# Moving the expert layer, the B, C and z products and the result products to other steps of the unit in a pipelined last stage

## The reference

```python
t = _unfold3(t, 2).transpose(0, 2, 1)          # taps of a 3x3 window, stride 2
h = t @ proj_w.T + proj_b                      # 768 channels

def _ssm_forward(x, A, W_B, b_B, W_C, b_C, W_D, b_D, p_Delta):   # x = layernorm(h)
    Bproj = x @ W_B + b_B                      # 16 states
    Cproj = x @ W_C + b_C
    delta = softplus(x @ W_D + b_D + p_Delta)  # x @ W_D is the "z product"
    A_bar = exp(delta[..., None] * A)
    B_bar = (A_bar - A) / (delta[..., None] * A) * delta[..., None] * Bproj[:, :, None, :]
    h = a * h + b * xl[..., None]              # per step of the sequence
    y = einsum('bn,bdn->bd', c, h)

route_prob = softmax((x @ enc_w + enc_b) @ sw_w + sw_b)   # x = layernorm(h) again, 8 experts
hid = gelu(einsum('td,edr->ter', x, w1) + b1) * onehot(argmax(route_prob))
out = (einsum('ter,erd->td', hid, w2) + onehot @ b2) * max(route_prob)
```

## Time and profile before

| what | value |
|---|---|
| runs | 9088.94, 9092.56, 9096.12 us; median 9092.56 |
| profiled execution | 9095.32 us, its span 9093.5 us |
| mean granted TensorE clock | 0.914 |
| PE busy | 7714.0 us, 85% |
| POOL busy | 6188.6 us, 68% |
| DVE busy | 6128.7 us, 67% |
| ACT busy | 4307.8 us, 47% |
| last stage, POOL's first product to the end of its last | 3644.8 to 8993.0 us |

### The profile page before, as it was taken

How to read it: one execution, slowest core, us unless ns; L and a number is a source line. 1 busy time by engine, 2 the same in 40 slices (tenths; PEclk the granted TensorE clock), 3 DMA queues, 4 the chain that set the end, 5 groups by cost and what they waited for, 6 DMA issues and landing times.

```text
span 9093.5 us, 86859 instructions
## 1 busy us (share of the span) xinstructions
PE 7714.0 (85%) x31228; PEld 3228.1 (35%) x31228; DVE 6128.7 (67%) x6499; ACT 4307.8 (47%) x7641; POOL 6188.6 (68%) x2484
## 2 busy tenths in 40 slices
PE   6799999876999996588888888788888888888887
PEld 4444444322434432133333333333333333333333
DVE  1255555542233333888888888888888888888885
ACT  1366666553344442444544445444445444454442
POOL 0011111115766640999999999999999999999995
PEclk8999999998999997699888998899998899988988
DMA  0011111113544432223333323233232332233331
GB/s 25 18 45 42 41 44 39 32 32 82 104 97 98 100 68 63 98 100 104 111 114 111 109 91 123 96 121 109 100 116 98 115 119 100 95 119 105 113 114 49
DMA packets 356855, 786.60 MB, mean 87 GB/s; under 512 B 70437, under 2 KB 282806, under 8 KB 348936
## 3 DMA queue, kind: packets, MB, share of 16 engines
q1 hardware_dynamic: 320376, 690.75, 24.9%
q0 software_dynamic: 21712, 51.75, 2.3%
q10 hardware_dynamic: 14336, 38.54, 1.2%
HBM read 597.36 MB, written 183.35 MB: 86 GB/s over the span
## 4 chain that ended last, share of the span: by engine, by line
PE 33%; DVE 14%; ACT 5%; issue 5%; POOL 3%; DMA 0%; SPq 0%; DVEq 0%; ACTq 0%; POOLq 0%
PE ps L1527 7%; PE ps L1635 6%; DVE v L1880 6%; DVE v L1871 5%; PE ps L1534 5%; PE ps L1532 5%; PE ps L1573 3%; ACT ps L1762 3%; PE ps L1523 2%; POOL v L1482 2%; PE ps L1638 2%; PE ps L1636 2%; POOL v L1494 1%; PE ps L1577 1%; DVE dl L1861 1%
## 5 line engine op out<-in xcount | busy, mean ns | idle before, releaser
L1880 DVE TENSOR_TENSOR_SCAN v<-ps,v 128x898 f32<-128x898 f32 x1344 | 2725.5, 2028 | 92.4
L1482 POOL TENSOR_TENSOR v<-xr,bt 128x1792 f32<-128x1792 f32 x672 | 2690.0, 4003 | 98.4 <-DMA xr<-h_by_channel 98.4
L1494 POOL TENSOR_TENSOR v<-v,ct 128x1792 f32<-128x1792 f32 x672 | 2475.4, 3684 | 239.6 <-ACT st L1723 238.9
L1762 ACT ACTIVATE ps<-dr,aa 128x448 f32<-128x448 f32 x2688 | 1586.0, 627 | 1554.8 <-DVE v L1880 1537.7
L1871 DVE SCALAR_TENSOR_TENSOR v<-ps,aa,v 128x448 f32<-128x448 f32 x2688 | 1691.2, 671 | 560.5 <-ACT ps L1762 501.0
L222 POOL DMA_DIRECT2D tokens<-ob x448 | 236.3, 534 | 1889.9 <-ACT ob L383 1839.1
L1635 PE MATMUL ps<-w_or_w,gm 128*112 128x384 f32 x1792 | 721.9, 552 | 369.7 <-DVE gm L1957 277.1
L1573 PE MATMUL ps<-v,dg 128*32 128x448 f32 x5376 | 705.1, 599 | 212.8 <-POOL v L1494 122.9
L1635 PEld LDWEIGHTS ps<-w_or_w,gm 128*112 128x112 f32 x1792 | 334.5, 197 | 768.5 <-DVE gm L1957 319.5
L1527 PE MATMUL ps<-h,w_or_w 128*128 128x448 f32 x1344 | 536.2, 549 | 16.6 <-DVE gm L1924 16.6
L1532 PE MATMUL ps<-x,wpa 128*128 128x448 f32 x1008 | 445.5, 577 | 17.3 <-ACT h L1688 10.1
(11 more groups left out here) (324 smaller groups left out, 11951.0 us busy)
## 6 DMA issues: line engine op xcount, KB each, us to landing
xr<-h_by_channel SPq DMA_DIRECT2D x168, 896.0 KB, 5.6
dr<-delta_by_channel SPq DMA_DIRECT2D x168, 896.0 KB, 6.3
x<-tokens SPq DMA_DIRECT2D x252, 224.0 KB, 5.3
tokens<-ob POOLq DMA_DIRECT2D x448, 112.0 KB, 2.4
w_or_w<-in_w SPq DMA_DIRECT2D x29, 1536.0 KB, 6.4
w_or_w<-centred_w SPq DMA_DIRECT2D x27, 1536.0 KB, 6.4
h_by_channel<-h SPq DMA_DIRECT2D x112, 336.0 KB, 10.9
delta_by_channel<-dl SPq DMA_DIRECT2D x112, 336.0 KB, 4.5
```

Source lines behind the costliest of these rows:

```text
L1482: tt(v[:, n % RING, :, 1:T + 1], xr[:, dc % 2], bt[:, q:q + 1, :].to_broadcast([128, 4, T]), ALU.mult).then_inc(s_v, 1)
L1494: tt(v[:, n % RING, :, 1:T + 1], v[:, n % RING, :, 1:T + 1], ct[:, q:q + 1, :].to_broadcast([128, 4, T]), ALU.mult).then_inc(s_cm, 1)
L1762: fn(decay(g), dr[:, dc % 2, g, :], ACT.Exp, scale=aa[:, 4 * k + g:4 * k + g + 1]).then_inc(s_a, 1)
L1880: nc.vector.tensor_tensor_scan(row, flat[:, 1024 * pair:1024 * pair + 2 * T + 2], row, 0.0, ALU.mult, ALU.add).then_inc(s_sc, 1)
```

## The change

No operation is added or removed. Thirty-odd numbers of the table change, and with them the step at which parts of `mlp` and `front` are issued, and three places in SP's loop. The taps (P_PJ, P_MU, A_HW, A_MU) stay where they are.

```diff
-        P_PJ, P_MU, P_VAR, P_Z, P_BC = 1, 7, (8, 10), 11, 9
-        A_HW, A_MU, A_SQ, A_RS, A_MX, A_SP = 5, 11, (9, 13), 14, (16, 17), (17, 18)
-        V_Z, V_BC, V_DL = 15, 14, (18, 19)
-        P_SQ, P_MEAN, P_ENC, P_IN, P_LOG, P_TURN = (0, 2), 1, 4, 5, 6, 10
-        P_MASK, P_OUT = (12, 13, 14, 15), (16, 17, 18, 18, 19, 20, 21, 22)
-        A_SQ2, A_MS, A_RS2, A_EX, A_GL = (2, 4), 5, 7, 11, 14
-        A_OUT = (21, 22, 23, 23, 24, 25, 26, 27)
-        V_VAR, V_ENC, V_IN, V_LOG, V_EQ, V_OH, V_MASK = 6, 8, 9, 10, 12, 14, (16, 17, 18, 19)
-        ROUTE, TAIL = 9, 28
+        P_PJ, P_MU, P_VAR, P_Z, P_BC = 1, 7, (8, 10), 12, 11
+        A_HW, A_MU, A_SQ, A_RS, A_MX, A_SP = 5, 11, (9, 13), 14, (17, 18), (18, 19)
+        V_Z, V_BC, V_DL = 16, 15, (19, 20)
+        P_SQ, P_MEAN, P_ENC, P_IN, P_LOG, P_TURN = (1, 3), 2, 5, 7, 7, 11
+        P_MASK, P_OUT = (14, 15, 16, 17), (18, 19, 20, 20, 21, 22, 23, 23)
+        A_SQ2, A_MS, A_RS2, A_EX, A_GL = (2, 5), 6, 8, 12, 16
+        A_OUT = (23, 24, 25, 25, 26, 27, 28, 28)
+        V_VAR, V_ENC, V_IN, V_LOG, V_EQ, V_OH, V_MASK = 7, 9, 11, 11, 13, 15, (18, 19, 20, 21)
+        ROUTE, TAIL = 9, 29
...
-                    if k == 11 and i >= 1:
+                    if k == 15 and i >= 1:
                         sp.wait_ge(s_hm, MT * i)
                         sp.dma_start(w2, w["w2"]).then_inc(s_wv, 16)
...
-                    if k == 19 and i + 1 < UNITS:
+                    if k == 20 and i + 1 < UNITS:
                         store_delta(i + 1)
-                    if k == 20:
+                    if k == 21:
                         spread(i + 1, 0)
```

## The result

| | before | after |
|---|---|---|
| median of 20 runs each | 9088.82 us (9078.29 to 9101.25) | 9117.12 us (9094.67 to 9126.33) |
| ratio | | 1.0027, 95% interval 1.0021 to 1.0033 |
| profiled execution, its span | 9095.32, 9093.5 us | 9110.96, 9109.2 us |
| first POOL product of the last stage to the end | 5448.7 us | 5470.1 us |
| unit, mean of units 2 to 26 | 191.73 us | 192.30 us |

The kernel is slower by 0.27%, 28 us by the medians; 9119 was forecast. The halves are means over 24 or 25 units, taken between the same instructions as in the prediction: the DVE half from the first weighing of step 12 (L1871) to the end of the fourth masking (L1957), the PE half from there to the end of the taps of the means, shown by ACT's copy behind them (L1691). The change moves 53 numbers of the table, more than the thirty-odd that are named above.

The account below looks back on a forecast made before the run. A ring of DVE and PE halves, not POOL, bounds the unit: 80.4 + 112.1 = 192.5 us against 191.7. 9095.3 + 20 (25 units) + 7 (edges) = 9122, less 2.8 to the median: 9119 us; range 9060 to 9165.

Parts of the forecast that it names:

- the DVE half: First weighing of step 12 to last masking on DVE: forecast 80.4 us a unit, 18.8 more than 61.6.
- the PE half: First result product to end of the means' taps: forecast 110.0 us, 112.1 with 2.1 to the weighing, 18.0 less.
- The ring: DVE half and PE half set the unit, 191.7 us before, 192.5 forecast; POOL's 9.3 us idle is left over.
- A: Rival: gaps at steps 12 and 13 go, nothing replaces them; unit 185.3, about 8930 us; with milder form 17%.
- B: Rival: no change, halves cancel or the clock wakes earlier; unit 191.3 to 192.1, -3 to +17 us; chance 28%.
- C: Rival: last C rows land late and put POOL in the ring at steps 5 to 7; 9195 us; chance 12%.
- The copies' waits: PE's fourth and fifth result products wait 0.6 and 1.1 us for ACT's copies, sums of squares none; before 3.43 and 2.57.
- The clock: PE's slow sums of squares go, slow first result product stays; one more slow product would cost 1.6 us a unit, +40.
- The wait at step 15: New DVE wait behind PE's fourth product with w1, second sums of squares and ACT's copy: 2.8 us a unit.
- the one at step 19: New DVE wait, as ACT's long delta functions sit right ahead of its copy L1751: 0.5 us a unit.
- The edges: Outside the repeating units: unit 1 starts step 12 7 us earlier, last expert layer begins 14 later, together +7 us.
- POOL's new waits: POOL waits some 3 us at step 0 for bt or xr, about 2 at step 5 for C rows, costing nothing.

Follow-up runs that it names:

- e1: Changed kernel with the last C rows issued ahead of the reload of w1, not behind it; ratio to before 1.0024, unit 192.29 us.
- e6: Changed kernel with xr and the first two B rows loaded ahead of the delta stores; ratio to before 1.0023, unit 192.31 us.
- e4: Kernel before with only the late last maskings and results of the change, first sums of squares in step 1; ratio 1.0197, unit 197.98 us.
- e3: Changed kernel with last maskings and results two steps earlier, delta at the changed steps; ratio to before 0.9893, unit 187.97 us.
- e9: e8 with the front's second sums of squares one step earlier, P_VAR (8, 9); ratio to before 0.9801, unit 184.33 us.
- e5: Changed kernel with the front's second sums of squares one step earlier, ahead of the fourth product with w1; ratio to before 0.9990, unit 191.15 us.
- e8: e3 with xr and the first two B rows loaded ahead of the delta stores; ratio to before 0.9828, unit 185.88 us.
- e10: e9 with ACT's third copy of the results at step 22 instead of 23; ratio to before 0.9793, unit 184.30 us.
- e11: e9 with the fourth to seventh result products a step later and their copies moved; ratio to before 0.9791, unit 184.22 us.
- e7: Changed kernel with results and last maskings one step earlier, and xr and B rows loaded ahead of the delta stores; ratio 0.9886, unit 187.42 us.

## Why the prediction was right

**The ring.** This was the step on which everything rested: POOL's idle time is left over, the two halves set the unit. Three runs bear it out directly. e1 and e6 each take away one of POOL's two new waits and the unit doesn't move (192.29 and 192.31 for 192.30); no run takes both away from the changed kernel at once. e4 lengthens the DVE half by 15.3 us (forecast 14.9) and shortens the PE half by 9.0 (forecast 7.8), and leaves POOL with 15.4 us of idle time a unit. Of the rivals, A (the gain arrives) had the gaps at steps 12 and 13 right, which vanish wholly; it failed in that nothing was to take their place. B (no change) failed narrowly: the unit is 0.2 us above its upper end of 192.1, and just inside the forecast's 192.2 to 193.5. C (the C rows decide) is what e1 refutes.

**The PE half, 110.0 forecast, 110.03 measured.** The sum is closer than its terms. The copies' waits are 0.73 and 1.15 for 0.6 and 1.1. The sums of squares wait 0.54 for ACT's last copy and were to wait nothing. The four L1577 take 3.4 for 3.8 and the two sums of squares 4.6 for 4.9, which makes up for it. In the 18.1 us by which the half is shorter than before, the two products with `w1` are the 9.3 of the prediction; the waits are 3.8 for 4.3, and the slow sums of squares 1.4 for 2.3, since the unit that was read was one of the slower ones. The first result product takes 6.59 us to the next instruction in the mean, where I had 6.02 and 0.5 for the clock, 6.52.

**The clock.** The granted clock in three windows of 30 us after the change (busy time of PE, PEld, DVE, ACT and POOL, then PEclk, DMA share and GB/s):

```profile
6530.00:6560.00 30.00, 29.46 (x107) 12.91 (x106) 25.79 (x24) 14.65 (x34) 27.34 (x8) 1.00 0.39 144
6660.00:6690.00 30.00, 12.56 (x30) 3.65 (x28) 29.45 (x32) 10.28 (x20) 27.34 (x8) 0.51 0.35 103
6690.00:6720.00 30.00, 28.13 (x129) 13.41 (x128) 24.87 (x25) 14.33 (x33) 28.05 (x8) 1.00 0.40 142
```

Around the expert layer's sums of squares it is 1.00, 2.4 GHz, where it was 0.89, which is 1.2 GHz for a fifth of those 30 us (the prediction read a tenth and more). Over the PE half some 10.3 us a unit were at 1.2 GHz before and 4.4 are after. Around the last masking it is 0.51, nearly all at 1.2 GHz, and PE has worked 12.56 of 30 us; it rises at the end of the first result product and stays. The pause ahead of that product is 14.2 us now and was 10.2, and the product takes as long (mean 6.59 for 6.52 us): the +40 us of a whole second product at half clock did not come. The Trainium skill (TensorE: Matmul & The Clock Gate, "The HAM clock gate") has the throttled state as the default that activity ends; by that rule a longer pause costs no more once the engine is throttled, and the trace agrees. The length of this pause doesn't order the other kernels either: behind 5.1 us the product takes 6.2 us in e3 and 7.2 in e9 (means), and what decides between these was not looked for.

**The DVE half, 80.4 forecast, 80.23 measured.** Two steps and the second write of delta are as read from the rows. The wait at step 15 is 2.77 for 2.8, the one at step 19 0.26 for 0.5. e5 shows the first to be on the path: with the sums of squares a step earlier the half loses 1.48 and the unit 1.15.

**The unit and the sum.** 192.30 for 192.5, so +0.57 a unit for +0.8. From the first weighing of step 12 of unit 1 to that of unit 26 this is +13.6 us where I had +20. The edges: unit 1 came 5.8 us earlier (forecast 7), the end moved by 13.6 (forecast 14). In the last stage +21.4 us for the forecast +27. The two spans differ by 15.7 us only, because the stages ahead took 5.7 us less in this profile; the medians of 20 runs, where their scatter averages out, differ by 28.3. Of the 28.3, the last stage of the two profiles accounts for 21.4; the forecast had 27 and stood on a median of 9092.56 from three runs, where twenty give 9088.82. That 9119 fell 2 us from the median of 9117.12 is closer than the terms deserve, and luck.

**POOL's new waits.** 3.9 us at step 0 in the mean (forecast some 3) and 3.3 at step 5 (forecast some 2; the sum took 16 us from the issue of the C rows to their use, the rows it names give 15.2, and with that the wait comes to 2.8), and 0.8 at step 16 with 1.0 and 0.8 at steps 18 and 23, which I had not named. The order in which SP issues them is as forecast; SP's timeline after the change:

```profile
6676.55 3.52 SPq L1366 DMA_DIRECT2D delta_by_channel<-dl  x4
...
6685.39 1.97 SPq L1402 DMA_DIRECT2D bt<-bc_rows  x3
...
6729.84 0.35 SPq L1446 DMA_DIRECT2D w_or_w<-centred_w  x1
6730.23 0.52 SPq L1402 DMA_DIRECT2D ct<-bc_rows  x1
```

The C rows leave 0.39 us behind `w1`, which waited for the last result product: as before the change. That made POOL wait and cost no time, since POOL had it to spare. In e3 it is otherwise for the B rows: POOL waits 5.4 us a unit for them there, and taking that away (e8) is worth 2.09 us a unit.

**What the change was worth in parts.** e3 and e8 keep the separation of taps and expert products and put the last masking where it was: 187.97 us a unit, and 185.88 with early loads, 3.76 and 5.85 less than before. So the separation is a gain, and the change lost it by moving the results two steps later along with it; e4 shows that part alone at +6.25. The best of these kernels (e9, e10 and e11 can't be told apart) take 0.979 to 0.980 of the time before, 173 to 198 us less.

## What to carry to other kernels

Where engines wait for each other in a ring across iterations, take one turn of it apart into its halves, and add up what an edit gives to each; as long as the busiest engine (here 95% busy) is not in the ring, its idle time is what the ring leaves over, and removing one of its waits only renamed it (e1, e6). The halves add up whatever the cause, so check inside each of them which engine is waited for. The edit that relieved one half here did so by pushing work later, and handed as much to the other, so move only what need not follow. And once the halves shrink, measure the waits again: the same early load was worth nothing at 192.3 us a unit (e6) and at 187.4 (e7), and 2.09 us in e3, where PE waited for POOL.

## What the runs showed that I had not expected

The stages ahead of the last one, the same in all kernels, ended anywhere from 3623.4 to 3652.2 us in thirteen profiles, while the mean unit of the last stage repeats to some hundredths of a microsecond (after, e1 and e6). And the ring did not stop at POOL's 182.3 us: three different kernels came to 184.33, 184.30 and 184.22, with POOL's last 2 us of idle time at step 0 in e9 and e10 and spread over three other steps in e11.
